# Fused cross-attention, self-attention and quantised layer: row fetches first in a round, ternary compares one round later, Hadamard column means through GpSimd

## The reference

```
x = x + cross(LN(x), ctx)    # 16 heads, latent 32: scores = (LN(x) Wq_d W_qk) . (ctx Wkv_d), softmax, V = C_kv Wv_u
x = x + selfattn(LN(x))      # one head of 128: qkv = LN(x) Wqkv + bqkv, softmax, Wo, + bo
x = x + ffn(LN(x)):
    xh    = LN(x) @ hadamard                      # 512 x 512
    scale = clip(max|xh|, 1e-5) / 7;  xq = clip(round(xh / scale), -8, 7) * scale
    ws    = clip(mean|weight| of a row, 1e-5)     # ternary weights, a scale per output
    wq    = (weight > 0.5 ws) - (weight < -0.5 ws), times ws
    out   = xq @ wq^T
```

## Time and profile before

| what | value |
|---|---|
| busy share of the span: PE, VectorE, ScalarE, GpSimd | 83%, 67%, 52%, 23% |
| chain that ended last: PE, VectorE, DMA, ScalarE | 37%, 22%, 13%, 10% |
| start of L698 in rounds 10, 11, 12, 13, 14 | 241.93, 262.06, 281.77, 301.04, 319.88 us |
| L652, eight matmuls, at 20.33 and at 47.76 us | 2.08 and 1.06 us |
| granted TensorE clock, 26.0 to 30.3, 30.3 to 37.6, 37.6 to 39.3 us | 0.77, 0.50, 0.71 |
| granted clock, 50.2 to 52.2, 52.2 to 54.0, 54.0 to 62.0, 62.5 to 64.0 us | 1.00, 0.51, 0.50, 1.00 |
| L698, L704, L712 in round 1 (low clock) | 2.82, 2.08, 1.91 us |
| L698, L704, L712 in round 8 | 1.90, 1.13, 1.05 us |
| wo_s, bo_row, w_rows, had_s, xr of pair 1: issue, us to landing | 8.06, 9.2; 7.10, 6.4; 7.58, 8.8; 12.94, 8.1; 12.23, 5.9 |
| ct of pair 1: issue, us to landing | 5.13, 5.5 |

### The profile page before, as it was taken

One profiled execution on the slowest core, in us unless ns is written; L12 is line 12 of the kernel. 1 busy time (PEld: TensorE's weight loads), 2 busy tenths in 40 slices (PEclk: granted clock), 3 DMA queues, 4 the chain that ended last, 5 costly groups with the idle time before them and its releaser, 6 DMA issues.

```text
span 374.9 us, 11411 instructions
## 1 busy us (share of the span) xinstructions
PE 312.1 (83%) x4603; PEld 206.3 (55%) x4618; DVE 251.0 (67%) x531; ACT 193.3 (52%) x628; POOL 84.9 (23%) x127
## 2 busy tenths in 40 slices
PE   4746969989797979798998989897989999968871
PEld 3436657656455565565665555655656666646520
DVE  1495743777686777677767858777776878765432
ACT  1350661937456474738383745647382939382210
POOL 2000200313131222213131312122231414131321
PEclk9995976999999999999999989999999999996997
DMA  7960020302002030303030200303031020000000
GB/s 240 315 258 2 25 90 3 112 31 112 30 12 108 30 112 30 112 28 112 28 112 28 88 32 19 112 28 112 30 113 60 2 60 0 31 2 30 2 28 28
DMA packets 13345, 25.37 MB, mean 68 GB/s; under 512 B 3200, under 2 KB 3712, under 8 KB 13312
## 3 DMA queue, kind: packets, MB, share of 16 engines
q1 hardware_dynamic: 13312, 24.91, 19.1%
HBM read 20.71 MB, written 4.19 MB: 66 GB/s over the span
## 4 chain that ended last, share of the span: by engine, by line
PE 37%; DVE 22%; DMA 13%; ACT 10%; issue 9%; POOL 5%; SPq 3%; POOLq 0%; DVEq 0%
DMA xr<-x_rows 12%; PE ps L698 9%; DVE mx L415 6%; PE ps L596 5%; PE ps L704 5%; PE ps L712 5%; POOL x2n L258 2%; PE ps L721 2%; DVE stat L444 2%; DVE stat L494 2%; PE ps L628 2%; ACT prob L298 2%; PE ps L621 2%; PE ps L688 2%; POOL rstd L255 2%
## 5 line engine op out<-in xcount | busy, mean ns | idle before, releaser
L295 ACT ACTIVATE prob<-ps,nmx,qk_scale 128x128 f32<-128x128 f32 x128 | 56.8, 457 | 36.5 <-DVE nmx L419 36.5
L605 PE MATMUL ps<-had_s,x3t 128*128 128x512 f32 x128 | 59.2, 605 | 1.4 <-ACT x3t L286 1.4
L298 ACT ACTIVATE prob<-ps,nmx,qk_scale 128x128 f32<-128x128 f32 x128 | 48.6, 491 | 0.0
L415 DVE TENSOR_REDUCE mx<-ps 128x8 f32<-128x1024 f32 x32 | 39.0, 1220 | 11.4 <-PE ps L596 11.4
L425 DVE STREAM_TRANSPOSE prob_t<-prob 128x1024 f32<-128x1024 f32 x32 | 39.0, 1220 | 2.0 <-ACT prob L298 2.0
L698 PE MATMUL ps<-prob_t,ckv_n 32*32 32x128 f32 x2048 | 34.1, 309 | 6.4 <-DVE prob_t L425 5.4
L605 PEld LDWEIGHTS ps<-had_s,x3t 128*128 128x128 f32 x128 | 23.0, 189 | 27.2 <-issue 25.4
L279 POOL TENSOR_TENSOR res<-prod,x 128x512 f32<-128x512 f32 x16 | 20.3, 1266 | 71.8 <-DVE prod L531 71.8
L638 PEld LDWEIGHTS ps<-x2t,wqkv_s 128*128 128x128 f32 x256 | 29.8, 191 | 10.2 <-ACT x2t L286 10.2
L638 PE MATMUL ps<-x2t,wqkv_s 128*128 128x128 f32 x256 | 32.8, 281 | 3.0 <-ACT x2t L286 1.4
L538 DVE SCALAR_TENSOR_TENSOR x<-ps,rsum,x2b 128x512 f32<-128x512 f32 x16 | 12.0, 751 | 32.3 <-PE ps L704 32.3
(11 more groups left out here) (109 smaller groups left out, 559.2 us busy)
## 6 DMA issues: line engine op xcount, KB each, us to landing
ct<-ctx_cols SPq DMA_DIRECT2D x16, 512.0 KB, 3.7
xt<-x_cols SPq DMA_DIRECT2D x16, 256.0 KB, 2.6
xr<-x_rows SPq DMA_DIRECT2D x16, 256.0 KB, 3.7
y<-res SPq DMA_DIRECT2D x16, 256.0 KB, 2.0
w_rows<-weight SPq DMA_DIRECT2D x1, 1024.0 KB, 8.8
had_s<-hadamard SPq DMA_DIRECT2D x1, 1024.0 KB, 8.1
wqkv_s<-wqkv SPq DMA_DIRECT2D x1, 768.0 KB, 9.7
wqk<-w_qk SPq DMA_DIRECT2D x2, 128.0 KB, 4.4
```

The source lines that it names most:

```text
L295: last = nc.scalar.activation(prob[:, h, :], score, ACT.Exp, bias=nmx[:, h:h + 1], scale=scale, accum_out=sum_a[:, h:h + 1])
L298: last = nc.scalar.activation(prob[:, h, :], score, ACT.Exp, bias=nmx[:, h:h + 1], scale=scale)
L415: V.tensor_reduce(mx[:, h], ps[:, 2 * half:2 * half + 2, :].rearrange("p r (c k) -> p (r c) k", c=EC), AX.X, ALU.max).then_inc(done["mx"], 1)
L605: mm = pe.matmul(ps[:, B4, :], x3t[:, c, :], had_s[:, c, :], start=(c == 0), stop=(c == EC - 1))
```

## The change

SyncE's queue: in a round the row load comes first, then the column loads, then the store. At the start the ternary layer's weights are loaded before the biases, the second row load stands ahead of wv_bd behind a wait for the second context tile, and the column loads of pair 2 stand ahead of wqkv.

Ternary: the scales stay in VectorE's round 0, the eight compares move to round 1, to the place where the subtraction of the Hadamard mean was.

Hadamard means: GpSimd adds the four row chunks of had_s up to one in round 0 (two instructions), TensorE multiplies that one chunk by mean_w in round 1 (one matmul call where there were four), ScalarE copies the result from PSUM, and GpSimd subtracts it from the four chunks in round 1, behind qk_scale. TensorE waits for the four subtractions ahead of the first Hadamard product, in round 2.

wide_scale (TensorE) and the copy to scale_row (ScalarE) of round 0 move ahead of the cross attention's value sums.

```
             load_cols(1, 1)
+            sp.dma_start(w_rows[:], weight.rearrange("(c p) n -> p c n", p=P)).then_inc(ld_w["w"], 16)
             for s in range(3):
                 sp.dma_start(b_qkv[:, s:s + 1], ...).then_inc(ld_w["b"], 16)
             sp.dma_start(bo_row[:], ...).then_inc(ld_w["b"], 16)
-            sp.dma_start(w_rows[:], weight.rearrange("(c p) n -> p c n", p=P)).then_inc(ld_w["w"], 16)
             sp.dma_start(wo_s[:], wo).then_inc(ld_w["wo"], 16)
+            sp.wait_ge(ld_ct[1], 16)
+            load_rows(1, 1)
             sp.wait_ge(zero_wv, 1)
             for r in range(4):
                 sp.dma_start(wv_bd[...], ...).then_inc(ld_w["wv"], 16)
-            load_rows(1, 1)
             sp.dma_start(had_s[:], hadamard.rearrange("(c p) n -> p c n", p=P)).then_inc(ld_w["had"], 16)
+            load_cols(2, 0)
             sp.dma_start(wqkv_s[:], wqkv.rearrange("(c p) n -> p c n", p=P)).then_inc(ld_w["wqkv"], 16)
-            load_cols(2, 0)

             def body(i, k, par, front, cross, self_, quant):
                 pre = isinstance(i, int)
+                if not pre or 1 <= i < PAIRS - 1:
+                    load_rows(i + 1, 1 - par)
+                if not pre or 0 <= i < PAIRS - 3:
+                    load_cols(i + 3, 1 - par)
                 if not pre or 3 <= i < PAIRS + 3:
                     store(i - 3, 1 - par)
-                if not pre or 0 <= i < PAIRS - 3:
-                    load_cols(i + 3, 1 - par)
-                if not pre or 1 <= i < PAIRS - 1:
-                    load_rows(i + 1, 1 - par)
...
 gpsimd, behind qk_scale:
+                if isinstance(i, int) and i == 0:
+                    pool.wait_ge(ld_w["had"], 16)
+                    nc.gpsimd.tensor_tensor(had_sum[:], had_s[:, 0:2, :], had_s[:, 2:4, :], ALU.add).then_inc(had_pair, 1)
+                    pool.wait_ge(had_pair, 1)
+                    nc.gpsimd.tensor_tensor(had_mean[:], had_sum[:, 0, :], had_sum[:, 1, :], ALU.add).then_inc(had_added, 1)
+                if isinstance(i, int) and i == 1:
+                    pool.wait_ge(hmean_read, 1)
+                    for c in range(EC):
+                        nc.gpsimd.tensor_tensor(had_s[:, c, :], had_s[:, c, :], had_sum[:, 0, :], ALU.subtract)\
+                            .then_inc(had_ready, 1)
 scalar, behind the copy of x2t:
+                if isinstance(i, int) and i == 1:
+                    act.wait_ge(hmean_made, 1)
+                    copy(had_sum[:, 0, :], ps[:, B4, :]).then_inc(hmean_read, 1)
 scalar: the copy to scale_row of round 0 moves from behind the copy of u_t to ahead of it
 vector:
                 if isinstance(i, int) and i == 0:
...
-                    ternary()
+                    ternary_scale()
                     dve.wait_ge(cb_made, 1)
                     V.tensor_tensor(const_row[:], ps[:, B4, :], bo_row[:], ALU.add).then_inc(const_ready, 1)
                 if isinstance(i, int) and i == 1:
-                    dve.wait_ge(hmean_made, 1)
-                    V.tensor_tensor(had_s[:], had_s[:], ps[:, B4, :]..., ALU.subtract).then_inc(had_ready, 1)
+                    ternary()
 tensor:
             def hadamard_mean():
-                pe.wait_ge(ld_w["had"], 16)
+                pe.wait_ge(had_added, 1)
                 pe.wait_ge(row_read, 1)
-                for c in range(EC):
-                    mm = pe.matmul(ps[:, B4, :], mean_w[:], had_s[:, c, :], start=(c == 0), stop=(c == EC - 1))
-                mm.then_inc(hmean_made, 1)
+                pe.matmul(ps[:, B4, :], mean_w[:], had_mean[:], start=True, stop=True).then_inc(hmean_made, 1)
 ternary_transposed(0) waits for hmean_read, not for had_ready
                     if first and i == 2:
                         pe.wait_ge(ternt_read, 2)
+                        pe.wait_ge(had_ready, EC)
                 if first and i == 0:
                     wide_bias()
+                    wide_scale()
 (and wide_scale() is taken out behind the cross output)
```

More of the change, by code:

```diff
@@ L53, in perceiver_kernel @@
         had_s = sb("had_s", [P, EC, E])
+        had_sum = sb("had_sum", [P, 2, E])
+        had_mean = sb("had_mean", [P, E])
         w_rows = sb("w_rows", [P, EC, E])
@@ L144, in perceiver_kernel @@
          tern_done, ternt_made, ternt_read, fold_made, wide_done, row_made, row_read, cb_made, const_ready, bvw_done,
-         hmean_made, had_ready) = [sem(n) for n in (
+         had_pair, had_added, hmean_made, hmean_read, had_ready) = [sem(n) for n in (
             "consts_set", "ident_set", "zero_wv", "mean_made", "wq_ready", "wabs_done", "wscale_done", "whalf_done",
             "neg_done", "tern_done", "ternt_made", "ternt_read", "fold_made", "wide_done", "row_made", "row_read",
-            "cb_made", "const_ready", "bvw_done", "hmean_made", "had_ready")]
+            "cb_made", "const_ready", "bvw_done", "had_pair", "had_added", "hmean_made", "hmean_read",
+            "had_ready")]
         made = {k: sem("made_" + k) for k in (
@@ L274, in body @@
                     after(pool, done["aux1"], i + 1)
-                    nc.gpsimd.tensor_tensor(qk_scale[:, 1 - par:2 - par], aux1[:], power[:], ALU.pow).then_inc(done["qk_scale"], 1)
+                    nc.gpsimd.tensor_tensor(qk_scale[:, 1 - par:2 - par], aux1[:], power[:], ALU.pow)\
+                        .then_inc(done["qk_scale"], 1)
+                if isinstance(i, int) and i == 0:
[8 more added lines that the diff above has]
+                            .then_inc(had_ready, 1)
                 if quant:
@@ L367, in body @@
                         .then_inc(ternt_read, 1)
+                if isinstance(i, int) and i == 0:
+                    act.wait_ge(row_made, 1)
+                    copy(scale_row[:], ps[:, B4, :]).then_inc(row_read, 1)
                 if cross:
@@ L372, in body @@
                          ps[:, 0:4, 0:P].rearrange("p b (c q) -> p b c q", c=EC)).then_inc(read["u"], 1)
-                if isinstance(i, int) and i == 0:
-                    act.wait_ge(row_made, 1)
-                    copy(scale_row[:], ps[:, B4, :]).then_inc(row_read, 1)
             looped(act, body)
@@ L390, in _, with ternary_scale @@
             V.tensor_copy(fold4[:], fold[:].unsqueeze(1).to_broadcast([P, 4, LAT])).then_inc(fold_made, 1)
-            def ternary():
+            def ternary_scale():
                 dve.wait_ge(ld_w["w"], 16)
@@ L400, in ternary @@
                 V.tensor_copy(w_wide[:], w_scale[:].unsqueeze(2).to_broadcast([P, EC, P])).then_inc(wide_done, 1)
+            def ternary():
                 dve.wait_ge(whalf_done, 1)
@@ L459, in body @@
                 if isinstance(i, int) and i == 1:
-                    dve.wait_ge(hmean_made, 1)
-                    V.tensor_tensor(had_s[:], had_s[:], ps[:, B4, :].unsqueeze(1).to_broadcast([P, EC, E]), ALU.subtract)\
-                        .then_inc(had_ready, 1)
+                    ternary()
                 if quant:
@@ L574, in ternary_transposed @@
                     pe.wait_ge(tern_done, EC)
-                    pe.wait_ge(had_ready, 1)
+                    pe.wait_ge(hmean_read, 1)
                 else:
@@ L713, in body @@
                     mm.then_inc(made["xo"], 1)
-                if first and i == 0:
-                    wide_scale()
                 if self_:
```

## The result

The changed kernel takes 359.52 us in the median (358.23 to 360.91, 4 runs), the kernel before 378.29 (377.73 to 382.33): the ratio is 0.948, 95% interval 0.940 to 0.956. The profiled execution took 358.43 us with a span of 356.6, against 376.65 and 374.9.

The account below looks back on a forecast made before the run. The late load of the next rows (xr), issued behind the column loads, was taken as the bound. Terms -13.1 - 2.13 + 0.12 + 1.1 = -14.0 us gave 362.6 profiled, median 364 us, range 360 to 369.

Parts of the forecast that it names:

- the control of rounds 13 and 14: Rounds without column loads, rows in time: round 14 takes 3.76 us from last five exponentials to value sums, round 12 4.63.
- the wait for p plus 0.15: Rounds 2 to 12: ScalarE's idle time before exponential p, 11.5 us in all, goes, plus 0.15 us a round.
- The store's new place: Each round: the store issued behind the column loads costs nothing, as its buffer is written again two rounds later.
- const_row waits for the bias product: Round 0: moving the compares frees 5.19 us, but const_row needs TensorE's bias product, so only 0.85 us come forward.
- the Hadamard additions and subtractions are hidden: Rounds 0 and 1: GpSimd's additions (3.8 us) and subtractions (5.1 us) finish before TensorE needs them; no time gained or lost.
- the compare beside x2b waits: Round 1: a VectorE compare waits for GpSimd's x2b through the shared port lock, between 0 and 1.28 us, taken as 1.1.
- Rows first: Rounds 2 to 12: the row load goes out about 7 us earlier, saving 13.1 us, bounds zero to about 19.
- rival (e): Better than forecast: the low clock of 52.2 to 62.5 us is avoided and no port wait occurs; 360 us, 12%.
- the term that was left at nothing: Rounds after 12 and the tail: the prediction's sum held no gain there, 0 us.
- Round 0 and 1: Set-up work moved: round 0 gives 2.13 us, round 1 costs 1.2 us.
- rival (b): TensorE stays at the low clock through the first half of round 1, 4 us longer, 368 us; 8%.
- signs of being wrong: A new ScalarE or TensorE wait of about 1 us a round, or granted clock falling in rounds where it stood at 1.00.

Follow-up runs that it names:

- e1: The kernel before with one edit: in each round the row load is issued first, then the column loads, then the store; 355.36 us, ratio 0.956.
- e1b: The kernel of e1, unedited, run again on one chip beside the changed kernel; 357.35 us, ratio 0.948.
- e2: The changed kernel with the old order in a round (store, column loads, row load), the rest kept; 378.47 us, ratio 1.015.
- e3: The changed kernel with the order store, row load, column loads in a round; 356.79 us, ratio 0.959.
- e4: The changed kernel with GpSimd's x2b of round 1 moved behind qk_scale; 356.58 us, ratio 0.957.
- e11: The kernel before with filler products (results unread) on TensorE, those in rounds placed ahead of its wait for qi_t; 376.87 us, ratio 1.003.
- e6: The kernel before with filler products (results unread) in TensorE's pauses, behind its wait for qi_t; 381.64 us, ratio 1.017.
- e9: The kernel of e1 plus wide_scale and its copy early, and one of four compare pairs moved to round 1; 356.08 us, ratio 0.943.
- e12: The kernel of e1 with filler products in the places of e7, 12 behind the bias product; 361.39 us, ratio 0.961.
- a2: The changed kernel, unedited, run again on one chip beside e1b; 358.45 us, ratio 0.951.
- e10: The changed kernel with fillers absent and the loads at the start in their old order; 359.16 us, ratio 0.956.
- e5: The changed kernel with all eight compares back in round 0, ahead of const_row; 357.90 us, ratio 0.950.
- e7: The changed kernel with filler products (results unread) on TensorE, 8 in round 0 behind the bias product; 353.60 us, ratio 0.943.

## Why the prediction was right and wrong

**The bound and the mechanism were right.** The rows were what the rounds waited for, the control of rounds 13 and 14 gave the new round (3.76 forecast, 3.75 measured from the exponentials to the value sums), the next limit is ScalarE, and e1, e1b and e2 show that this one step carries the whole gain. In the five loop rounds that no low spell touches (5 to 8 and 11) the gain was 6.26 us, where the wait for p plus 0.15 gives 6.30. The store's new place costs nothing (e3). const_row waits for the bias product, the Hadamard additions and subtractions are hidden, and the compare beside x2b waits (1.59 us; 0.48 in e4).

**What failed is the size, in two terms; neither counts what a late load does to TensorE's clock.** The first is the step *Rows first*: "I take 13.1, as the control is the same round without the late load", with bounds up to 19. From L716 of round 1 to that of round 12 the changed kernel gained 14.3. The seven rounds of the loop gained 9.5, not 8.7, and all of the surplus is in rounds 9 and 10, around the low spell at 218 us (3.25, where waits and 0.15 give 2.38); round 1 to 2 gained 2.2, not 1.0, and at the loop's entry 0.8 was lost. The surplus is time at the low clock, into which the kernel before falls near such waits and the changed kernel does not, or for less long. The spell at 218 us on the page of the kernel before, and in the columns used above:

```profile
PEclk9995976999999999999999989999999999996997
...
218.00:222.00 4.00, 3.01 (x54) 1.72 (x66) 3.84 (x10) 1.75 (x7) 0.55 (x1) 0.69 0.00 0
```

The prediction had this as rival (e) and gave it 12% and 2.7 us for the spell of round 1, with no wait of the compare beside it. Its 360 is the number nearest to the measured one, but by luck: the wait of the compare was there, and the spell got shorter and did not go. e1 and e1b, without the rest of the change, do lose the spell with the rows (6.0 us in rounds 1 and 2 where 2 were due). In the profiles with late rows TensorE's clock fell in the middle of the kernel (62 to 315 us) at 218 us (before), at 74, 118 and 262 us (e2), at 138 us (e11), and at 76 and 142 us (e6): in all four. In the twelve with rows in time it did so in three (at 92 to 98 us in e1b and e9, at 116 us in e12), each time at the loop's entry, where also those of e2 at 118, e11 at 138 and e6 at 142 us stand. Away from the entry it fell in three of the four, and in none of the twelve. The mean granted clock of all executions points the same way: 0.945 (45 of the kernel before) and 0.936 (e2), against 0.949 to 0.963 for the kernels with rows in time and no fillers.

The second is the term that was left at nothing: everything behind round 12. It gave 2.7 us of the profiled pair, 2.5 of them in the tail, by a shorter low spell. That is mostly chance. From the value sums of round 15 to the end it is 32.9 us without a low spell there (e3), 33.4 to 33.7 with one of 3.4 us (the changed kernel, a2, e1) and 35.6 to 35.9 with one of 6.8 us (before, e2, e1b, e4, e9, e10; e5 does not fit, 35.3 with 3.4); and e1 and e1b are the same kernel. Chance in one profile cannot make the medians differ by 18.8 us, though, and in the second set the difference was 18.9 again (377.35 to 358.45). There the runs' mean granted clock gives a hint. Among executions with a mean clock of 0.950 to 0.955, the seven of the kernel before have a median of 373.6 us and the six of the changed kernel 358.5: 15 us apart, near the forecast's 14; the other 3 to 4 us of the 18.8 go with the lower clock at which the kernel before usually runs. This is a correlation over several chips and not an experiment. The experiment on it did not confirm it: holding the clock up in the kernel before gained nothing (e11), in the changed kernel 5 us (e7), and e11 was hit by issue stalls and later rows at once. So the cause of the missing 4.5 us in the medians is argued, not shown.

**What the rest of the change did.** Round 0 and 1 were to give 0.9 us. In the profile up to L716 of round 1 it is 1.28. But against rows first alone on one chip the whole change is level or 1 us behind: the value sums of round 0 start no earlier in a2 than in e1b (29.11 and 29.05 us), and round 1 is 2.6 us longer (25.53 against 22.96), with the compare beside x2b and with a clock that falls at 41 us, where in e1b the Hadamard products kept TensorE busy. That is rival (b), the low clock in round 1, to which the prediction gave 8%: it did occur (41 to 45 us), and with it one of the prediction's own signs of being wrong, a clock that falls where it had stood at 1.00. What it cost by itself no run isolates; e5, with both low spells and without the compares in round 1, is 1.2 us longer there than e1b, so 4 us were too much.

**The range** was too narrow on the fast side. It ended at the 360 of rival (e), which took the spell of round 1 and the compare's wait as the only good luck, though the page of the kernel before shows two more spells in its clock row, at 218 and at 338 us.

## What to carry to other kernels

A transfer should not stand in an in-order queue behind one that waits for something later than its own buffer: reordering three issues gave the whole 5% here, and four careful moves of set-up work beside it gave nothing that could be measured. Rounds of the trace that lack the wait in question price such a change better than the sum of the waits; to that belongs what the pause does to TensorE's clock, since a wait that lets it fall can be paid twice. Work moved into another engine's or another round's gap should be checked against what runs beside it there.

## What was not expected of the hardware

- A load of 256 KB behind 768 KB of others lands 3.7 us after its issue in the median (kernel before); issued ahead of them it takes 2.7 (changed kernel). In e6 one was used only 5.9 us after its issue. Late in a queue it is both slower and less even.
- A VectorE compare of 512 columns took 1.59 us beside a GpSimd addition and 0.48 us without it. The Trainium skill, page "SBUF — State Buffer", section "SBUF: two separate sides", tells of this exclusive lock, and the prediction counted on it; on the blocking the traces agree. By the recorded starts the compare began 0.04 us before the addition and yet was the one that waited, where that section gives the ports to whichever starts first; as the spans on GpSimd are rough, the order of the two is not settled.
- Around the entry of the hardware loop (rounds 3 and 4) TensorE stalls amid its value sums with nothing to wait for in the trace: 0.96 us in the kernel before, 1.47 in the changed one, 1.21 in its second profile, 1.86 in e3, 0.21 in e5, 1.43 in e11, 1.51 in e1b and none in e1, which is the same kernel. 13 of the 16 profiles have it. Its cause is open.
- Filler products that cost 0.3 us in each loop round made the changed kernel 5 us faster, with the clock held at 2.4 GHz (mean granted clock 0.98 to 0.99 where it was 0.94 to 0.96). The same fillers made the kernel before 6.5 us slower (e6) and the rows-first kernel 4 us slower (e12): they pay only where they stand off the path and the clock would have fallen.
